# Output rows stored by SP, a subtraction folded into POOL's scaling, and four residual sums made early

## The reference

```python
B, N, D = 4, 1024, 512; heads = 16; hd = 32
def _sln(h, w):      # layer norm with gain and bias made from the condition w
    ln = (h - mean(h)) / sqrt(var(h) + 1e-5) * ln_g + ln_b
    return (w @ Wg.T + bg)[:, None, :] * ln + (w @ Wb.T + bb)[:, None, :]
h = _sln(hidden, w)
q, k, v = split(h @ Wqkv.T + bqkv)             # 16 heads of 32
att = softmax(q @ k.T, axis=-1) / D ** 0.5
out = (att @ v) @ Wp.T + bp
h1 = out + hidden
return _sln(h1, w) + h1                          # fp32, 4 x 1024 x 512
```

## Time and profile before

| | |
|---|---|
| median of the runs | 1386.43 us |
| profiled execution, its own time | 1391.84 us |
| span of the profile, first to last instruction | 1390.2 us |
| busy: PE, DVE, POOL, ACT | 93%, 77%, 76%, 51% |
| iterations 1 to 3 (tiles, no outputs) | 72.0 us each |
| iterations 6 to 8 (tiles and outputs) | 77.5 us each |
| iterations 12 and 13 (bare) | 70.3 and 70.1 us |

### The profile page before, as it was taken

One profiled execution on the slowest core, in us unless ns is written; L12 is line 12 of the kernel. 1 busy time (PEld: TensorE's weight loads), 2 busy tenths in 40 slices (PEclk: granted clock), 3 DMA queues, 4 the chain that ended last, 5 costly groups with the idle time before them and its releaser, 6 DMA issues.

```text
span 1390.2 us, 33206 instructions
## 1 busy us (share of the span) xinstructions
PE 1294.5 (93%) x9988; PEld 904.0 (65%) x9988; DVE 1065.7 (77%) x1754; ACT 702.4 (51%) x1374; POOL 1062.6 (76%) x755
## 2 busy tenths in 40 slices
PE   7898999999999999999999999999989898989993
PEld 4897676767676767676776767677545555555562
DVE  5345788888888888787888878787968788887535
ACT  4221355555565556455555556555545555555341
POOL 1444176767676799899898999997897989898845
PEclk9899899999999999999999999999999999999997
DMA  7578534443444545446454635437453434243321
GB/s 245 144 209 228 126 94 115 116 115 107 106 122 109 150 116 162 105 144 152 125 148 114 174 93 159 105 116 159 123 134 84 116 84 113 83 114 92 89 55 64
DMA packets 216708, 174.13 MB, mean 125 GB/s; under 512 B 105493, under 2 KB 186517, under 8 KB 216633
## 3 DMA queue, kind: packets, MB, share of 16 engines
q1 hardware_dynamic: 214456, 166.83, 45.0%
q0 software_dynamic: 1984, 6.29, 1.2%
q10 hardware_dynamic: 192, 0.07, 0.0%
HBM read 113.29 MB, written 58.51 MB: 124 GB/s over the span
## 4 chain that ended last, share of the span: by engine, by line
PE 39%; POOL 27%; issue 17%; POOLq 6%; DVE 6%; DMA 2%; SPq 1%; ACT 1%; DVEq 1%; ACTq 0%
POOL p L1658 15%; PE ps_o L852 7%; PE ps_st L835 6%; PE ps_a L821 5%; PE ps_w L784 4%; PE ps_w L726 4%; POOLq L1513 4%; PE ps_st L784 3%; DVE half_max L1367 2%; PE ps_s L865 2%; POOL y_t L1568 2%; POOL p_far L1658 2%; POOLq L1515 2%; POOL y_t L1570 1%; POOL h_tile L1531 1%
## 5 line engine op out<-in xcount | busy, mean ns | idle before, releaser
L1130 ACT ACTIVATE p<-ps_st 128x512 f32<-128x512 f32 x864 | 485.8, 599 | 434.4 <-PE ps_st L835 395.4
L1658 POOL TENSOR_TENSOR p<-p 128x1024 f32<-128x1024 f32 x208 | 532.0, 2558 | 144.2 <-PE ps_o L852 133.7
L1367 DVE TENSOR_REDUCE half_max<-ps_a 128x1 f32<-128x512 f32 x729 | 483.5, 684 | 120.6 <-PE ps_a L821 116.8
L835 PE MATMUL ps_st<-q_stack,k_stack 98*128 98x512 f32 x1024 | 419.1, 411 | 8.5 <-ACT p L1130 3.5
L821 PE MATMUL ps_a<-k_stack,q_stack 96*128 96x512 f32 x729 | 310.2, 428 | 15.0 <-DVE half_max L1367 11.9
L835 PEld LDWEIGHTS ps_st<-q_stack,k_stack 98*128 98x128 f32 x1024 | 197.6, 193 | 70.3 <-ACT p L1130 39.8
L852 PE MATMUL ps_o<-p,v_head 128*32 128x256 f32 x3456 | 210.7, 384 | 0.0
L821 PEld LDWEIGHTS ps_a<-k_stack,q_stack 96*128 96x128 f32 x729 | 139.9, 193 | 94.5 <-issue 40.3
L1367 DVE TENSOR_REDUCE half_max<-ps_st 128x1 f32<-128x512 f32 x231 | 158.3, 685 | 29.3 <-PE ps_st L821 28.8
L784 PEld LDWEIGHTS ps_w<-hT_s,wqkv_s 128*128 128x128 f32 x1056 | 157.5, 190 | 20.2
L852 PEld LDWEIGHTS ps_o<-p,v_head 128*32 128x32 f32 x3456 | 110.9, 111 | 79.3 <-issue 7.2
(11 more groups left out here) (201 smaller groups left out, 1433.6 us busy)
## 6 DMA issues: line engine op xcount, KB each, us to landing
qk_scratch<-qkT_s SPq DMA_DIRECT2D x108, 256.0 KB, 2.4
q_stack<-qk_scratch SPq DMA_DIRECT2D x192, 128.0 KB, 2.6
k_stack<-qk_scratch SPq DMA_DIRECT2D x192, 128.0 KB, 2.8
x_tile<-in_x SPq DMA_DIRECT2D x34, 256.0 KB, 4.9
gq_s<-gain_bias_scratch SPq DMA_DIRECT2D x16, 512.0 KB, 4.2
v_scratch<-v_parts SPq DMA_DIRECT2D x32, 256.0 KB, 3.5
v_head<-v_scratch SPq DMA_DIRECT2D x64, 128.0 KB, 2.1
att_scratch<-o_stage SPq DMA_DIRECT2D x240, 32.0 KB, 1.5
```

The lines of the kernel that those rows point to most:

```text
L835: pe.matmul(ps_st[:, (ST_BANK_WIDE if wide else ST_BANK)[2 * k + e], :], k_stack[0:98, s, k * 128:(k + 1) * 128], q_stack[0:98, s, e * 512 ...
L1130: nc.scalar.activation(p_of(step // 8, tiles)[:, k, e * 512:(e + 1) * 512], ps_st[:, (ST_BANK_WIDE if tiles else ST_BANK)[2 * k + e], :], ...
L1367: V.tensor_reduce(half_max[:, s % 2, item:item + 1], A_BANK[bank], AX.X, ALU.max).then_inc(a_used, 1)
L1658: G.tensor_tensor(p[:, 4 * h + 3, :], p[:, 4 * h + 2 - j % 2, :], p[:, 4 * h + 3, :], ALU.add).then_inc(pair_added, 1)
```

## The change

1. POOL no longer issues the stores of the output rows. SP stores them (store_y): at steps 6 and 13 of the next iteration, and in the last iteration at steps 8, 13, 22, 28. Each waits on out_pool for POOL's last addition on that tile. Two small DMAs on POOL at the start become semaphore increments.
2. power no longer makes the negative mean; the scaling (h_tile and y_t) takes the mean with subtract instead of add.
3. In iterations 1 to 4 POOL adds bp to x_tile of pairs 7 to 10 into y_t (keep_residual, steps 17 and 21, each behind the pair_add of that step) and SP stores it to a DRAM tensor (steps 23 and 27). In iterations 11 to 14 SP loads these rows into res_t, in place of rows of x, and POOL's additions at steps 15 and 16 go; DVE's out_sum waits for the load.
4. In the last iteration SP's wait for POOL and the load of go_s go from step 5 to step 10, behind the reciprocals' store, and POOL's two residual additions go ahead of the last two scale-and-finish parts of the pair before.

```diff
@@ -70,7 +70,6 @@
 OUT_LOW_STEP = {23: 0, 27: 1}
 OUT_HIGH_STEP = {22: 0, 25: 1}
 
-RESIDUAL_BARE = {15: 0, 16: 1}
 OUT_NORM_BARE = {19: 0, 20: 1}
 OUT_HIGH_BARE = {21: 0, 22: 1}
 OUT_LOW_BARE = {23: 0, 24: 1}
@@ -80,6 +79,9 @@
 RECIP_STORE_STEP = 10
 RESIDUAL_LOAD_STEP = 1
 OUT_LOAD_STEP = 14
+Y_STORE_STEP = {6: 0, 13: 1}
+KEEP_STEP = {17: 0, 21: 1}
+KEEP_STORE_STEP = {23: 0, 27: 1}
 
 
 def conditioned_attention(nc, x, cond, ln_g, ln_b, Wg, bg, Wb, bb, Wqkv, bqkv, Wp, bp, out):
@@ -101,13 +103,14 @@
 
     x_rows = x.rearrange("b n d -> (b n) d")
     out_rows = out.rearrange("b n d -> (b n) d")
+    out_pairs = out_rows.rearrange("(t a p) d -> t a p d", a=2, p=128)
 
     qk_d = nc.dram_tensor("qk_scratch", [4, B, D, N], F32, kind="Internal").ap()
     v_d = nc.dram_tensor("v_scratch", [NV, 128, N // 128, HD], F32, kind="Internal").ap()
     att_d = nc.dram_tensor("att_scratch", [B, D, N], F32, kind="Internal").ap()
     rcp_d = nc.dram_tensor("rcp_scratch", [B, H, N], F32, kind="Internal").ap()
     gb_d = nc.dram_tensor("gain_bias_scratch", [PAIRS, 2, D], F32, kind="Internal").ap()
-    mark_d = nc.dram_tensor("mark_scratch", [2, 1, 16], F32, kind="Internal").ap()
+    res_d = nc.dram_tensor("residual_scratch", [PAIRS, 2, 128, D], F32, kind="Internal").ap()
     att_heads = att_d.rearrange("b (h d) (e n) -> (b h) e d n", d=HD, e=4)
     att_tiles = att_d.rearrange("b (c p) (t n) -> b t p c n", p=128, n=128)
     rcp_heads = rcp_d.rearrange("b (c s) (p j) -> (b c) p s j", s=4, p=128)
@@ -239,6 +242,8 @@
         res_in = [sem(f"res_in{s}") for s in range(2)]
         go_in = sem("go_in")
         res_ready = sem("res_ready")
+        res_kept = sem("res_kept")
+        kept_out = [sem(f"kept_out{a}") for a in range(2)]
         scale_in = [sem(f"scale_in{s}") for s in range(2)]
         out_normed = sem("out_normed")
         out_hi = sem("out_hi")
@@ -274,6 +279,8 @@
 
         LAST = ITERS - 1
         LATE = END - 1
+        KEPT = LAST_TILES - FIRST_OUTS
+        BARE = LAST - LAST_TILES
         PRE_LOAD_STEP = {11 + 2 * t: t for t in range(8)}
         PRE_NORM_STEP = {13 + 2 * t: t for t in range(8)}
         PRE_HIGH_STEP = {14 + 2 * t: t for t in range(8)}
@@ -282,6 +289,7 @@
         PRE_ADD_STEP = {17 + 2 * t: t for t in range(8)}
         ACC_LOAD_STEP = {2: 0, 3: 1, 5: 2, 6: 3, 12: 4, 15: 5, 16: 6, 18: 7}
         ACC_ADD_STEP = {9: (0, 1), 10: (2, 3), 20: (4,), 22: (5,), 24: (6,), 26: (7,)}
+        LATE_STORE_STEP = {8: (LATE - 1, 0), 13: (LATE - 1, 1), 22: (LATE, 0), 28: (LATE, 1)}
         LATE_MM_STEP = {10: 0, 12: 1}
         LATE_SUM_STEP = {11: 0, 13: 1}
         LATE_HIGH_STEP = {5: 0, 6: 1}
@@ -547,6 +555,22 @@
                     sp.dma_start(scale_t[32 * s:32 * s + 32, a],
                                  part[:, :, s].rearrange("b t c n -> (b t) c n").to_broadcast([32, DC, 128])
                                  ).then_inc(scale_in[a], 16)
+
+            def store_y(pair, a):
+
+                sp.wait_ge(out_pool, 10 * pair + 5 * a + 5 + ONE)
+                sp.dma_start(out_pairs[bass.ds(pair, 1), a].rearrange("b p d -> (b p) d"), y_t[:, a, :]).then_inc(y_out[a], 16)
+
+            def store_kept(pair, a):
+
+                sp.wait_ge(res_kept, 2 * (pair - KEPT) + a + 1)
+                sp.dma_start(res_d[bass.ds(pair, 1), a].rearrange("b p d -> (b p) d"), y_t[:, a, :]).then_inc(kept_out[a], 16)
+
+            def load_kept(pair, a):
+
+                sp.wait_ge(kept_out[a], 16 * BARE)
+                sp.wait_ge(out_summed, 2 * pair + ONE)
+                sp.dma_start(res_t[:, a, :], res_d[bass.ds(pair, 1), a].rearrange("b p d -> (b p) d")).then_inc(res_in[a], 16)
 
             def load_residual(pair, a):
 
@@ -625,7 +649,7 @@
             for a in range(2):
                 store_v(LEAD - 1, a)
 
-            def iteration(i, tiles, norms, outs, first=False, last=False, gather=False):
+            def iteration(i, tiles, norms, outs, first=False, last=False, gather=False, late=True, keep=False):
                 pair = i - FIRST_OUTS
                 for s in range(4):
                     u = 4 * i + s
@@ -655,16 +679,25 @@
                             store_fin(u - 1, (s + 3) % 4)
                         elif k == 7 and not (first and s == 0):
                             store_sums(u - 1, (s + 3) % 4)
+                        if outs and late and not last and step in Y_STORE_STEP:
+                            store_y(pair - 1, Y_STORE_STEP[step])
+                        if last and step in LATE_STORE_STEP:
+                            store_y(*LATE_STORE_STEP[step])
                         if outs and step == RESIDUAL_LOAD_STEP:
                             for a in range(2):
-                                load_residual(pair, a)
+                                if tiles or last:
+                                    load_residual(pair, a)
+                                else:
+                                    load_kept(pair, a)
+                        if keep and step in KEEP_STORE_STEP:
+                            store_kept(i + LEAD + 1, KEEP_STORE_STEP[step])
                         if step == RECIP_STORE_STEP and not first:
                             store_recips(i - 1)
                         if last and step == 0:
                             for a in range(2):
                                 load_att(pair, a)
                                 load_scale(pair, a)
-                        if last and step == 5:
+                        if last and step == 10:
 
                             sp.wait_ge(out_pool, 10 * pair + ONE)
                             load_gain(go_s, go_in, pair)
@@ -690,8 +723,9 @@
 
             iteration(0, True, True, False, first=True)
             with sp.Fori(1, FIRST_OUTS) as i:
-                iteration(i, True, True, False)
-            with sp.Fori(FIRST_OUTS, LAST_TILES - 1) as i:
+                iteration(i, True, True, False, keep=True)
+            iteration(FIRST_OUTS, True, True, True, late=False, keep=True)
+            with sp.Fori(FIRST_OUTS + 1, LAST_TILES - 1) as i:
                 iteration(i, True, True, True)
             iteration(LAST_TILES - 1, True, False, True)
             iteration(LAST_TILES, False, False, True, gather=True)
@@ -1293,11 +1327,14 @@
                 p = p_of(s, near)
                 V.tensor_tensor(p[:, 4 * h + 1, :], p[:, 4 * h, :], p[:, 4 * h + 1, :], ALU.add).then_inc(slab_added, 1)
 
-            def out_sum(pair, a):
+            def out_sum(pair, a, mode):
 
                 P = 2 * pair + a
                 dve.wait_ge(out_projected, P + 1 + OUT_BEFORE)
-                dve.wait_ge(res_ready, P + 1)
+                if mode == "bare":
+                    dve.wait_ge(res_in[a], 16 * pair + 16)
+                else:
+                    dve.wait_ge(res_ready, P + 1 - (2 * BARE if mode == "last" else 0))
 
                 dve.wait_ge(out_pool, 10 * pair + ONE)
                 V.tensor_tensor(h1_t[:, a, :], ps_w[:], res_t[:, a, :], ALU.add).then_inc(out_summed, 1)
@@ -1448,7 +1485,7 @@
                             recips(i - 1)
                         if outs:
                             for a in sums:
-                                out_sum(pair, a)
+                                out_sum(pair, a, mode)
                                 if last:
                                     out_stats(2 * pair + a, a)
                         if last and step in PRE_ADD_STEP:
@@ -1504,12 +1541,11 @@
             pool.wait_ge(id_ready, 1)
 
             for a in range(2):
-                G.dma_start(mark_d[a], ident[0:1, 0:16]).then_inc(y_out[a], 16)
+                pool.sem_inc(y_out[a], 16)
 
             def power(mv, std, chain):
 
                 G.tensor_tensor(std[:, 1:2], mv[:, 1:2], eps_s[:, 0:1], ALU.add)
-                G.tensor_tensor(std[:, 0:1], zero_s[:, 0:1], mv[:, 0:1], ALU.subtract)
                 pool.drain()
                 G.tensor_tensor(std[:, 1:2], std[:, 1:2], minus_half[:, 0:1], ALU.pow).then_inc(chain, 1)
                 pool.drain()
@@ -1520,7 +1556,7 @@
 
                 need(pool, tile_mm, 8 * (pair - 1) + a + 1)
                 power(mv_t[:, a, :], std_t[:, a, :], ln_pool)
-                G.tensor_scalar(h_tile[:, a, :], x_tile[:, a, :], std_t[:, a, 0:1], std_t[:, a, 1:2], ALU.add, ALU.mult
+                G.tensor_scalar(h_tile[:, a, :], x_tile[:, a, :], mv_t[:, a, 0:1], std_t[:, a, 1:2], ALU.subtract, ALU.mult
                                 ).then_inc(ln_pool, 1)
 
             def norm_gain(pair, a):
@@ -1548,14 +1584,20 @@
                 pool.wait_ge(res_in[a], 16 * pair + 16)
                 G.tensor_tensor(res_t[:, a, :], res_t[:, a, :], bp_s[:], ALU.add).then_inc(res_ready, 1)
 
+            def keep_residual(pair, a):
+
+                need(pool, kept_out[a], 16 * (pair - KEPT))
+                G.tensor_tensor(y_t[:, a, :], x_tile[:, a, :], bp_s[:], ALU.add).then_inc(res_kept, 1)
+
```

(23 more changed lines are left out.)

## The result

The changed kernel takes **1410.17 us** (median of 4 runs, 1407.5 to 1412.4) against 1386.45 us: a ratio of **1.0162** (95% interval 1.0143 to 1.0182). It is 24 us slower. The forecast was 1386.0, with a range up to 1392.0, so both were wrong; so was every rival, the slower one too. The profiled execution spans 1410.6 us where that of before spans 1390.2, so the traces show 20.4 of the 24 us.

A forecast was written before the change was run, and what follows sets the result against it. PE sets the time with tiles; bare iterations hold 7.8 us of PE waits each. Terms 5.5 - 3.9 + 3.0 - 4.6 = 0.0 left the median 1386.43 at 1386.4, stated as 1386.0, range 1367 to 1392.

The forecast's parts named there:

- minus the subtraction removed, 0.14 us: Iterations 1 to 4: 0.14 us credited for the removed subtraction against the early residual addition's 1.35 us.
- a subtraction twice: Iterations 5 to 9: two subtractions leave POOL's path; with one store of 1.32 us, 1.6 us on paper.
- part 1: Iterations 1 to 4: early residual sums on POOL delay PE, +5.5 us, bounds 0 and +10.
- part 2: Iterations 5 to 9: POOL's relief gives 0.5 us each, plus 1.4 us of clock in iteration 5: -3.9 us.
- part 3: Bare iterations 12 to 14: PE's wait moves from POOL to SP's row, clock falls behind it: +3.0 us.
- part 4: Last iteration: SP's later wait frees the sums, removing DVE's 8.21 us wait and PE's idle time: -4.6 us.
- A: Rival, bare iterations: SP doesn't hold the row, POOL's relief reaches the end, 14.1 us gained: 1369; chance 0.25.
- B: Rival, bare iterations: the wait moves to the row but the clock holds: 1381.6 us; chance 0.13.
- C: Rival, slower: whole clock loss behind the row, +6.8 for +3.0, and +2 in early iterations: 1391.8; chance 0.2.

The follow-up runs named there:

- e1: The changed kernel with the folded subtraction alone undone (POOL subtracts separately, scales by add and multiply): 1384.14 us, ratio 0.9974.
- e9: e5 with the early residual additions at steps 10 and 11 in place of 17 and 21, behind a wait for the tile: 1361.87 us, ratio 0.9798.
- e5: e1 with SP's second-tile store (step 13) and output-gains load (step 14) moved to step 22 in bare iterations: 1366.23 us, ratio 0.9846.
- e8: The kernel before with SP's wait for POOL and output-gains load at step 10, not 5, in the last iteration: 1384.55 us, ratio 0.9975.
- e3: The kernel before, scaling still add and multiply, mean read from the statistics tile, separate subtraction kept: 1389.9 us in one run.
- e10: e5 with the folding of the subtraction into the scaling put back: 1395.26 us, ratio 1.0046.

## Why the prediction was wrong

**The step that failed** is in parts 1, 2 and 3 alike: "minus the subtraction removed, 0.14 us" and "a subtraction twice". I priced the instruction that goes and left the one that stays at its old length, although the diff gives it another operation. No row of before shows a POOL scaling with a subtraction, so its price was unknown and needed bounds; it got neither a bound nor a rival. The rows carry what it costs: 1.31 us more in each scaling, 2.08 against 0.77. Two scalings an iteration make +2.6 us on POOL in iterations 1 to 3, and four make +5.2 us in 5 to 9. Set into the sum by e1 against the changed kernel, this term is +26 us; the forecast had it as a gain. The rest of the sum comes out within 4 us.

**The other steps** can be judged on e1, which has all of them and not this one. Its shift against the trace of before is -3.9 us where I had 0.0. By the first table it is made up so:

| stretch | forecast | e1 |
|---|---|---|
| up to step 0 of iteration 1 | 0 | +0.3 |
| part 1, to step 24 of iteration 4 | +5.5 | +5.7 |
| part 2, to step 24 of iteration 9 | -3.9 | -5.1 |
| part 3, to step 24 of iteration 14 | +3.0 | 0.0 |
| part 4, to the end | -4.6 | -4.8 |

- Part 1: right. The wait at step 20 was forecast at 1.4 us and is 1.29, the period at 73.2 and is 73.06; the second addition in iteration 4, put at +0.7, cost 1.3 (PE waits 1.22 us at step 24). e9 shows that the cause is the place between the two additions.
- Part 2: the mechanism was right, the size a little small. The period was forecast at 77.0 and is 76.95, so 0.6 us came of the 1.6 on paper, and iteration 5 gave another 1.5 by its clock, as forecast. The rest of the difference is mostly iteration 5, whose shorter waits gave 1.1 us where I had 0.5. The prediction said that DVE's addition would wait for POOL's and then hold up the pair_add by about 1.1 us. In e1 DVE's addition, begun inside POOL's residual one, takes 1.80 us in place of 1.22, and ends 1.1 us into the two pair_adds behind, which take 5.86 us in place of 4.87. First POOL in before, then POOL and DVE in e1:

```profile
629.49 4.87 POOL L1658 TENSOR_TENSOR p<-p 128x1024 f32<-128x1024 f32 x2
```
```profile
629.91 1.29 POOL L1586 TENSOR_TENSOR res_t<-res_t,bp_s 128x512 f32<-128x512 f32 x1
631.16 5.86 POOL L1699 TENSOR_TENSOR p<-p 128x1024 f32<-128x1024 f32 x2
```
```profile
630.47 1.80 DVE L1328 TENSOR_TENSOR p<-p 128x1024 f32<-128x1024 f32 x1
```

- Part 3: the wait moves from POOL to the row, as forecast (3.20, 2.07 and 2.84 us in iterations 12 to 14), and the clock falls behind it (0.50, 0.56 and 0.50 in the 3 us behind). e5 shows by removal that SP's loop holds the row. Iterations 12 to 14 alone cost +0.9 us, not +3.0. The falls weren't cheap: PE is busy 190.6 us in them where e5, with a whole clock, has 183.7, which is 6.8 us. But before is busy 189.3 us: its clock fell behind step 16 (0.63 in the 3 us behind, in iteration 12), where e1 has 1.00. I hadn't set these falls against the new ones. Net the clock cost 1.2 us, and PE's idle time went from 21.5 to 21.2. The other -0.9 lies in iterations 10 and 11, and a single trace can't carry it: e8, whose code is that of before up to the last iteration, stands at -0.1 us at step 16 of iteration 11 and at -3.0 at its step 24. Against e8 part 3 comes to +2.9.
- Part 4: right. e8 alone shows -4.2 us in its trace and -3.5 by its ratio.

Single traces of the same code thus differ by 3 us in the bare iterations, so that the split of the -3.9 holds to that only; the total agrees with the ratio, 0.9974.

**The rivals.** A, in which POOL's relief reaches the end, was given 1369. It doesn't happen in this change, but it is what e5 does once SP's loop is cut: 1366, with 13.2 us gained in iterations 12 to 14 where A had 14.1, and 7 more in 11 that A didn't have. B, in which the clock holds behind the row, is ruled out by e1's 0.50. C, slower, had the right sign but not the cause: it named the clock behind the row, at most 1392, and that mechanism is present in e1, which is faster than before. With the 26 us, which only the runs gave, one can say what a bound would have been worth. Had the unknown length of the scaling been bounded from below by its old 0.77 us and from above by POOL's dearest row with two operands of that shape, 1.56 us (h_tile by gq_s, L1533, mean of 32), the upper end would have risen by 0.79 / 1.31 of 26 us, 16 us, to 1408: near the result, though even this bound lies below 2.08.

## What to carry to other kernels

When a change merges an instruction into another, price the one that remains: it is a new form, and if no row of the trace has its operations, its cost is unknown on both sides, whatever the shape says. A wait that an engine's queue carries for another engine is paid by everything queued behind it; moving SP's store and load behind the row gave 18 us. And the worth of a part depends on what else holds the path: the early sums cost 2 to 5 us beside one wait and saved 13 us without it, so parts are tested together as well as alone.

## What the hardware showed

- POOL's scaling with two scalars, 128x512 in f32, takes 0.77 us for add and multiply, multiply and add, and multiply and multiply; it takes 2.08 us for every pair tried with a subtraction and for add and add. With one operation it takes 1.57 us, more than a fast pair. The Trainium skill, GPSIMD Engine Reference, section Elementwise — side-by-side cycle accounting, gives 769 ns as measured for 512 elements in a tight loop, as the best case and without naming the operations. The fast pairs, 768 ns, agree with it in the total; the slow ones, at 2.08 us, are no such best case. The two widths don't agree with it: they give 0.9 ns per element, where the page's 1.8 cycles at 1.2 GHz would be 1.5 ns, an estimate from that page.
- Where the scalar of the mean comes from doesn't matter: 0.77 us with both scalars from one tile (before) and from two (e3).
- DVE's addition of 128x1024, 1.22 us by itself, took 1.80 us when it began inside one of POOL's, and POOL's two behind it 5.86 us in place of 4.87 (e1 against before, iteration 6).
- Waits of PE of 1.29 us (e1, step 20 of iterations 1 to 3) left the granted clock at 1.00. Waits of 2.00 to 2.01 us at the same step were followed by 3 us at 0.59, 0.54 and 0.50 in iterations 1, 2 and 3 of the changed kernel and at 1.00 in its iteration 4; in e10 it was the other way round, 1.00 in iterations 1 and 2 and 0.63 and 0.58 in 3 and 4. At that length of wait these traces don't tell in advance whether the clock falls.
